# One attention in another order of its heads, and the last stage of the last sequence in two halves

## The reference

```python
# layer 0: causal attention (16 heads of 16), feed-forward with exact gelu, gate
x1 = x + attn(layernorm(x)) @ Wo + bo
x  = x + g * (x1 + gelu(ln(x1) @ W1 + b1) @ W2 + b2 - x)
# layer 1: adapter with an expert chosen per sequence;  layer 2: feed-forward with an expert chosen per sequence
# layer 3: attention with a bias and a mask for every head, then a feed-forward
x = ln(x) * (1 + scale) + shift                  # scale, shift from the timestep
scores = q @ k.T / 4 + attention_bias            # bias: [4, 16, 512, 512] fp32
probs  = softmax(where(src_mask, -inf, scores))
x = x + (probs @ v) @ Wo + bo
h = ln(x) * g2 + beta2
x = x + gelu2(h @ W1 + b1) @ W2 + b2             # W1: 256 x 1024, W2: 1024 x 256; gelu2(z) = z * sigmoid(1.702 z)
```

## Time and profile before

| | |
|---|---|
| three timed runs | 1167.12, 1172.2 and 1169.03 us, median 1169.03 us |
| the profiled execution | 1163.56 us, its span 1161.5 us |
| busy in the span | PE 997.7 us (86%), DVE 730.8 us (63%), ACT 694.2 us (60%), POOL 454.1 us (39%) |
| chain that ended last | PE 51%, DVE 18%, ACT 15%, issue 9%, DMA 4%, POOL 4% |
| HBM | 132 GB/s over the span |
| granted TensorE clock | mean 0.959 of full speed |

### The profile page before, as it was taken

How to read it: one execution, slowest core, us unless ns; L and a number is a source line. 1 busy time by engine, 2 the same in 40 slices (tenths; PEclk the granted TensorE clock), 3 DMA queues, 4 the chain that set the end, 5 groups by cost and what they waited for, 6 DMA issues and landing times.

```text
span 1161.5 us, 22288 instructions
## 1 busy us (share of the span) xinstructions
PE 997.7 (86%) x7668; PEld 658.7 (57%) x7668; DVE 730.8 (63%) x1964; ACT 694.2 (60%) x1608; POOL 454.1 (39%) x694
## 2 busy tenths in 40 slices
PE   4878889897889898798889998897996899799768
PEld 3435557465556575466546565575573557557545
DVE  5677773737755738846773668638649864764750
ACT  3566564664675755676565755656754775675731
POOL 8300020000530374561072006847737564894920
PEclk8899999998999998899999999899897899999989
DMA  6868425133261634854626128575393387944600
GB/s 175 224 157 187 74 73 113 34 84 62 63 140 46 146 122 127 198 177 149 130 75 148 37 90 209 183 166 194 104 226 104 121 225 224 219 141 150 214 1 19
DMA packets 118354, 154.79 MB, mean 133 GB/s; under 512 B 12956, under 2 KB 80924, under 8 KB 118244
## 3 DMA queue, kind: packets, MB, share of 16 engines
q1 hardware_dynamic: 113636, 147.04, 47.3%
q0 software_dynamic: 1936, 3.97, 1.4%
q10 hardware_dynamic: 2672, 2.36, 0.6%
HBM read 134.47 MB, written 18.88 MB: 132 GB/s over the span
## 4 chain that ended last, share of the span: by engine, by line
PE 51%; DVE 18%; ACT 15%; issue 9%; DMA 4%; POOL 4%; DVEq 0%; ACTq 0%; POOLq 0%
PE bank L1307 14%; PE bank L1296 9%; PE bank L1399 7%; PE bank L1258 5%; PE bank L1413 5%; PE bank L1381 4%; POOL bias L798 4%; DMA bias<-in_fside_Bx16xSxS 3%; DVE mrow L1142 3%; ACT gT L874 3%; DVE bias L1148 3%; ACT bias L827 2%; ACT prob L824 2%; ACT L874 2%; ACT L827 2%
## 5 line engine op out<-in xcount | busy, mean ns | idle before, releaser
L798 POOL TENSOR_TENSOR bias<-bias,negmask 128x256 f32<-128x256 f32 x512 | 335.9, 687 | 259.2 <-DMA bias<-in_fside_Bx16xSxS 252.6
L827 ACT ACTIVATE bias<-bias,mrow 128x512 f32<-128x512 f32 x256 | 184.1, 719 | 209.3 <-DVE mrow L1148 207.8
L1148 DVE CUSTOM_DVE_ANT_0 bias<-bank,bias 128x512 f32<-128x512 f32 x256 | 175.4, 687 | 186.5 <-PE bank L1381 175.3
L824 ACT ACTIVATE prob<-bank,mrow 128x128 f32<-128x128 f32 (+3 forms) x256 | 134.7, 527 | 193.1 <-DVE mrow L1142 191.6
L1142 DVE TENSOR_REDUCE mrow<-bank 128x1 f32<-128x128 f32 (+3 forms) x256 | 124.5, 488 | 164.5 <-PE bank L1384 163.1
L1381 PE MATMUL bank<-ks,qs 128*128 128x512 bf16 (+3 forms) x512 | 180.3, 352 | 49.2 <-ACT prob L824 34.5
L1399 PE MATMUL bank<-ident,bias 128*128 128x128 f32 x1024 | 164.7, 286 | 54.0 <-ACT pT L835 43.8
L1399 PEld LDWEIGHTS bank<-ident,bias 128*128 128x128 f32 x1024 | 125.2, 146 | 123.9 <-ACT bias L827 71.3
L1296 PE MATMUL bank<-hT,w 128*128 128x512 f32 x384 | 182.6, 606 | 2.0 <-ACT hT L851 0.9
L1307 PE MATMUL bank<-w,gT 128*128 128x256 f32 x768 | 174.3, 381 | 0.0
L1307 PEld LDWEIGHTS bank<-w,gT 128*128 128x128 f32 x768 | 142.5, 190 | 20.2 <-issue 2.7
(11 more groups left out here) (155 smaller groups left out, 1140.6 us busy)
## 6 DMA issues: line engine op xcount, KB each, us to landing
bias<-in_fside_Bx16xSxS SPq DMA_DIRECT2D x128, 512.0 KB, 4.6
w<-in_L_cond_W SPq DMA_DIRECT2D x16, 1024.0 KB, 5.6
qs<-q_parts SPq DMA_DIRECT2D x30, 384.0 KB, 10.3
ks<-k_parts SPq DMA_DIRECT2D x30, 384.0 KB, 11.7
q_parts<-parts SPq DMA_DIRECT2D x80, 128.0 KB
k_parts<-parts SPq DMA_DIRECT2D x48, 128.0 KB
w<-in_L_cond_Wi SPq DMA_DIRECT2D x4, 1024.0 KB, 5.0
w<-in_L_cond_Wo SPq DMA_DIRECT2D x4, 1024.0 KB, 5.6
```

The lines of the kernel that those rows point to most:

```text
L798: pool.tensor_tensor(b_n, b_n, negmask[:, t, keys], ALU.add).then_inc(masked, 1)
L824: act.activation(prob_of(U), score_bank[U % 2][:, 0:n], ACT.Exp, bias=mrow[:, U % ROW_RING:U % ROW_RING + 1], accum_out=rsum[:, U % ROW_RI ...
L827: act.activation(prob_of(U), prob_of(U), ACT.Exp, scale=-1.0, bias=mrow[:, U % ROW_RING:U % ROW_RING + 1], accum_out=rsum[:, U % ROW_RING: ...
L1148: v.tensor_tensor_reduce(out=prob_of(U), in0=score_bank[U % 2][:], in1=prob_of(U), scale=-1.0, scalar=3e38, op0=ALU.add, op1=ALU.min, accu ...
```

## The change

The last attention goes through its batches as (c 0, tiles 0-1), (c 1, tiles 0-1), (c 1, tiles 2-3), (c 0, tiles 2-3). So `ctxn` of tiles 0 and 1, all heads, is complete 39 ticks after its start. A new plan, `plan_half`, does projection, norm, turn and `hidden` with gelu for tokens 0 to 255 from tick 488 on (448 + 40), beside the rest of the attention, and the same for tokens 256 to 511 from tick 520 on (448 + 72). The products with W2 of the first half come at ticks 521 and 522, behind the second projection. They go to three PSUM banks that the attention used. Stores are three, on SP's queue: tiles 0-1, tile 2, tile 3. SP issues the second `stack` of attention 7 at tick 449. The mask tiles 2 and 3 are turned when batch 2 comes to them.

```diff
+LAST_ATT = len(ATTENTIONS) - 1
+LAST_ORDER = [(0, 0), (1, 0), (1, 2), (0, 2)]
+HALF_AT = [40, 72]
+def plan_half(t, s, i):
+    at(t, "pe", "project", s, 1, i)
+    at(t + 1, "v", "residual", s, 1, i)
+    at(t + 2, "v", "stats", s, 6, i)
+    for r in range(RSQRT_STEPS):
+        at(t + 3 + r // SLOTS, f"v{r % SLOTS}", "rsqrt", s, 6, r, i)
+    at(t + 6, "v", "apply", s, 6, i)
+    at(t + 7, "p", "res_l3_half", s, i)
+    at(t + 7, "pe", "turn_half", s, i)
+    at(t + 8, "v", "feature_cols", s, i)
+    at(t + 8, "a", "feature_cols", s, i)
+    t += 10
+    ahead = (0, 0, 1, 3, 4, 5, 7, 8) if i else range(NF)
+    behind = (1, 1, 1, 5, 5, 5, 8, 8) if i else range(1, NF + 1)
+    for j, (dt, da) in enumerate(zip(ahead, behind)):
+        at(t + dt, "pe", "hidden_cols", s, i, j)
+        at(t + da, "a", "gelu_cols", s, i, j)
+    if i == 0:
+        t = UNITS * LAST_ATT + HALF_AT[1]
+        for x in range(2):
+            at(t + 1 + x, "pe", "ff_out", s, 2, x)
+        at(t + 9, "v", "ff_add", s, 2, 0)
+        at(t + 10, "sp", "store_part", s, 0)
+    else:
+        for x in range(2):
+            at(t + 9 + x, "pe", "ff_out", s, 2, 2 + x)
+            at(t + 10 + x, "v", "ff_add", s, 2, 1 + x)
+            at(t + 11 + x, "sp", "store_part", s, 1 + x)
-STACKS_AT = [(-2, 11)] + [(-28, 4)] * 2 + [(-20, 4)] + [(-28, 4)] * 3 + [(-20, 4)]
+STACKS_AT = [(-2, 11)] + [(-28, 4)] * 2 + [(-20, 4)] + [(-28, 4)] * 3 + [(-20, 1)]
-    [(9, norm(6), 3), (15, block3, 3)],
+for _i, _t in enumerate(HALF_AT):
+    plan_half(UNITS * LAST_ATT + _t, LAST_SEQ, _i)
-A_LOAD = {"feature_half": 7, "hi": 7, "mid": 7, "gelu": 10, "down": 20, "expert": 6}
+A_LOAD = {"feature_half": 7, "feature_cols": 4, "hi": 7, "mid": 7, "gelu": 10, "gelu_cols": 8, "down": 20, "expert": 6}
...
             c, t, e, j = u // (2 * NT * GH), u // (2 * GH) % NT, u // GH % 2, u % GH
+            if a == LAST_ATT:
+                c, t = LAST_ORDER[u // BATCH][0], LAST_ORDER[u // BATCH][1] + u // (2 * GH) % 2
...
+            def store_part(s, i):
+                sp.wait_ge(ff_done, 2 * FFN[s, 2] + i + 1)
+                tt = LAST_TILES[i]
+                sp.dma_start(out[s].rearrange("(t p) d -> p t d", p=P)[:, tt, :], xy[s][:, tt, :]).then_inc(stored, 16)
...
+            def res_l3_half(s, i):
+                pool.wait_ge(tok[5], NT * NTH[s, 5] + 2 * (i + 1))
+                for t in (2 * i, 2 * i + 1):
+                    res(pool.tensor_tensor(xy[s][:, t, :], xy[s][:, t, :], b2[1][:], ALU.add))
+                res_landed()
...
-                    if c == 0 and e == 0 and j == 0:
+                    if e == 0 and j == 0 and (c, t) in ([(0, 0), (0, 1), (1, 2), (1, 3)] if a == LAST_ATT else [(0, x) for x in range(NT)]):
...
+            def gelu_cols(s, i, j):
+                n, cols = FFN[s, 2], slice(HALF * i, HALF * (i + 1))
+                act.wait_ge(f1_psum, NF * (n + i) + j + 1)
+                act.activation(gT[:, j, cols], dense_bank[FF_BANK[j]][:, cols], ACT.Gelu_apprx_sigmoid,
+                               bias=b1[2][:, j:j + 1]).then_inc(g_done, 1)
...
             def ff_add(s, f, i):
+                if (s, f) == (LAST_SEQ, 2):
+                    tt = LAST_TILES[i]
+                    psum = pairs(last_bank[i])[:, 0:tt.stop - tt.start, :]
+                    v.wait_ge(res_pool, res_count(s, 3, min(i, 1)))
...
+            def turn_half(s, i):
+                dense_banks_free(issued)
+                pe.wait_ge(wo_done, 2 * LAST_ATT + i + 1)
+                for t in (2 * i, 2 * i + 1):
+                    pe.wait_ge(tok[5], NT * NTH[s, 5] + t + 1)
+                    for c in range(ND):
+                        mm = pe.transpose(dense_bank[c][:, t * P:(t + 1) * P], h[:, t, c * P:(c + 1) * P], ident[:])
+                mm.then_inc(t_psum, 1)
+            def hidden_cols(s, i, j):
+                n, cols = FFN[s, 2], slice(HALF * i, HALF * (i + 1))
...
+                if j >= 3:
+                    pe.wait_ge(g_done, NF * (n + i) + j - 2)
+                for c in range(ND):
+                    mm = pe.matmul(dense_bank[FF_BANK[j]][:, cols], w1[:, c, j * P:(j + 1) * P], hT[:, c, cols],
+                                   start=c == 0, stop=c == ND - 1)
+                mm.then_inc(f1_psum, 1)
+            def last_out(s, t):
...
+                    pe.wait_ge(max_done, ALL_UNITS)
+                    copied(ALL_UNITS)
+                for j in range(NF):
+                    if t % 2 == 0:
+                        pe.wait_ge(g_done, NF * (n + t // 2) + j + 1)
+                    mm = pe.matmul(last_bank[i][:, (t == 1) * D:((t == 1) + 1) * D],
+                                   gT[:, j, t * P:(t + 1) * P], w2[:, j, :], start=j == 0, stop=j == NF - 1)
...
             def project(s, l, i):
-                if i == 0:
+                if ATT[s, l] == LAST_ATT:
+                    dense_banks_free(issued)
+                    if i:
+                        pe.wait_ge(g_done, NF * (FFN[s, 2] + 1))
+                    pe.wait_ge(ctx_norm, BATCHES * LAST_ATT + 2 * (i + 1))
...
-                if U == 2 * HH or U % (UNITS // 2) == 0 and U:
+                if U == 2 * HH or U % UNITS in ((0, BATCH) if a == LAST_ATT else (0, UNITS // 2)) and U:
                     pe.wait_ge(stack_in[hd // HH], 96 * (a + 1))
```

More of the change, by code:

```diff
@@ L246, in plan_loads @@
 def plan_loads():
-    ffns = sorted((first_tick("pe", "hidden", s, f), s, f) for s in range(B) for f in range(3))
+    ffns = sorted((first_tick("pe", "hidden_cols" if (s, f) == (LAST_SEQ, 2) else "hidden", *((s,) if (s, f) == (LAST_SEQ, 2) else (s, f))), s, f)
+                  for s in range(B) for f in range(3))
     for n, (_, s, f) in enumerate(ffns):
@@ L289 @@
 TURN = order("pe", "turn_tokens", lambda a: a)
+TURN[LAST_SEQ, 5] = len(TURN)
 NTH = {(s, k): sum(1 for x in TURN if x[1] == k and TURN[x] < n) for (s, k), n in TURN.items()}
+NTH[LAST_SEQ, 5] = sum(1 for x in TURN if x[1] == 5) - 1
 FFN = order("pe", "hidden", lambda a: a[:2])
+FFN[LAST_SEQ, 2] = len(FFN)
 QKV = order("pe", "qk", lambda a: a[:2])
@@ L522, in res_count @@
                                            if e == "p" and st.startswith("res")):
-                total += NT * (2 if step == "res_l0" else 1)
+                total += {"res_l0": 2 * NT, "res_l3_half": NT // 2}.get(step, NT)
                 if step == name and args[0] == s:
+                    return total
+                if step == "res_l3_half" and (s, layer) == (LAST_SEQ, 3) and args[1] == half:
                     return total
@@ L852, in feature_half, with feature_cols @@
                                    bias=norm_w[w][:, 2:3]).then_inc(hT_a, 1)
+            def feature_cols(s, i):
+                cols = slice(HALF * i, HALF * (i + 1))
+                act.wait_ge(t_psum, TURN[s, 5] + 1 + i)
+                act.activation(hT[:, 0, cols], dense_bank[0][:, cols], ACT.Identity, scale=norm_w[2][:, 0:1],
+                               bias=norm_w[2][:, 2:3]).then_inc(hT_a, 1)
             def hi(s, l, i):
@@ L1000, in _, with rsqrt @@
             chain = [0]
-            def rsqrt(s, k, i):
+            def rsqrt(s, k, i, half=None):
                 var, bits, guess, sq = nwt[:, 0, :], nwt[:, 1, :], rstd, nwt[:, 2, :]
@@ L1007, in rsqrt @@
                 if i == 0:
-                    for t in range(NT):
+                    tiles = range(NT) if half is None else range(2 * half, 2 * half + 2)
+                    for t in tiles:
                         count[0] += 1
                         ins = v.bn_aggr(mv[:, t, :], stats[:, t, :])
-                        if t < NT - 1:
+                        if t < tiles[-1]:
                             ins.then_inc(vec, 1)
@@ L1170, in normalize @@
                 a, b = divmod(p, BATCHES)
-                c, t = b // 2, b % 2 * 2
+                c, t = LAST_ORDER[b] if a == LAST_ATT else (b // 2, b % 2 * 2)
                 if b == 0 and a:
@@ L1284, in project @@
                 mm.then_inc(wo_psum, 1)
-                if i == 1:
+                if i == 1 and ATT[s, l] != LAST_ATT:
                     issued["out"] += 1
@@ L1427, in _ @@
             steps = dense_steps("pe")
-            do = {"turn_tokens": turn_tokens, "qk": qk, "v": v_rows, "project": project, "hidden": hidden,
+            do = {"turn_tokens": turn_tokens, "turn_half": turn_half, "hidden_cols": hidden_cols, "qk": qk, "v": v_rows, "project": project, "hidden": hidden,
                   "ff_out": ff_out, "turn_expert": turn_expert, "down": down, "expert": expert, "up": up, "setup": setup, "restack": restack}
```

45 lines of the change are left out of this document (34 added, 11 removed).

## The result

The changed kernel took 1185.3 us (median of four runs, 1176.27 to 1190.37) beside 1168.07 us for the kernel before on the same chip: ratio 1.0135, 95% interval 1.0077 to 1.0193. Six more runs in the first experiment gave 1181.95 us, ratio 1.0114 (1.0090 to 1.0139). Forecast were 1172.5 us and a range of 1164 to 1180, so the loss, 13.5 to 17 us, is four to five times the forecast 3.6. The profiled execution took 1176.27 us with a span of 1174.5, 13.0 us more than before.

The account below looks back on a forecast made before the run. It took POOL's mask additions to bound the last attention, with nothing overlapping in the 46.5 us behind it. Terms 1.5 + 22.2 - 0.5 - 19.6 + 0 = +3.6 us; on the median 1172.5 us, range 1164 to 1180.

Parts of the forecast that it names:

- The table loads of the middle: Ticks 499 to 506: one gelu a tick beside an exponential, eight Gelu and eight Exp loads; added 22.2 us, bounds 21.3 and 23.8.
- rival 4: Each of the 16 table loads holds ACT once more for its own length, 1.28: +20.5 us, 1193; chance 0.03.
- rival 3: Tables don't switch tick by tick; gelus grouped as in sequence 2, three load pairs for eight: -12.8 us, 1160; chance 0.05.
- The tail: From the last ctxn to the end of the span: 19.6 us saved, some 2.9 of it from the clock.
- The order and the mask tiles: Last attention: the two mask tiles move to ticks where POOL waits for bias anyway; cost 0.
- Ticks 488 to 498: First half's projection, norm, transposes and hT beside the last attention: cost 1.5 us, POOL's two additions; bounds 0 and 5.
- DVE gets about 5 us: DVE's added work in ticks 488 to 498, against slack of 3.3 and copies worth 2.3 going to ACT: it fits.
- PE gets about 1.8 + 1.0, within its slack over 11 units: PE's added projection and transposes in ticks 488 to 498 fit its slack of some 0.3 us a unit.
- Ahead of it: Second stack of attention 7 issued at tick 449, not 452, some 4 us sooner: cost 0, bounds -4.3 and +2.
- Rival 2: Earlier stack removes POOL's 4.29 us bias wait, so sequence 2's stage begins sooner: -2.2 us in all, 1166.8; chance 0.16.
- rival 1: Low clock: half-idle PE in the eight slow ticks leaves the last units and tail's start at 1.2 GHz: 1177.5; chance 0.28.
- The base: Sum 1167.2 us against the profiled execution, plus 5.5 by which the median of timed runs exceeded it: 1172.6.

Follow-up runs that it names:

- the first experiment: The changed kernel timed again with nothing altered, to see how far its runs lie apart: 1181.95 us, ratio 1.0114 to the kernel before.

## Why the prediction was wrong

*The table loads of the middle*: right. The step had 22.2 us, the trace has 21.5; with three pairs in place of eight 14.8 us went (13.2 of them in units 499 to 507). A load has no drain behind it (1110.62 to 1111.91, 1.29 us), so rival 4 falls, and rival 3 as well.

*The tail*: right, 19.6 us in both, clock included. *The order and the mask tiles*: right, nothing.

*Ticks 488 to 498*: wrong, 1.5 against 7.8 us (5.7 to 7.8 in nine profiles), and the upper bound of 5 too low. Three steps failed:

- "DVE gets about 5 us", and with it "So DVE's sum fits". I took DVE's durations from the earlier trace rows, the norm behind the attention, where POOL stands still, and put them beside a POOL that is busy 27.2 of 28 us. With POOL kept quiet DVE's busy time in this stretch grew by 2.4 us (11.97 to 14.35), which is the 5 less the 2.3 of the copies; with POOL at work it grew by 5.4 (to 17.41). That put 3.0 us on the path. I looked at each engine's slack alone, not at two engines that slow each other.
- "PE gets about 1.8 + 1.0, within its slack over 11 units". The projection is one lump at one tick, and 1.8 us of it stood on the path in every kernel that has it there. The prediction itself had said that a lump on one engine doesn't fit.
- The clock in these ticks was not in the sum at all. Behind the norm it was low in the first profile and cost some 2.1 us.

*Ahead of it*: wrong, 0 with bounds -4.3 and +2 against +3.5 in the profile, and +4.1 between the means of seven and six profiles. The failing step is "I take 0, since the bytes stay the same", with the +2 that bounds "pairs held up ahead of it can lengthen another". The stack went 5.9 us sooner (992.32 for 998.20), where I had some 4. The bytes did stay the same and the pair behind the stack came as late as before after its issue, but it was now the pair of unit 458, for which DVE stood waiting: 1.9 us in this profile, up to 4.9 in others; what makes it vary so is not shown. The wait of 4.29 us that "An earlier start can shorten" had cost little where it was, since DVE did most of the norm of sequence 2 under it, at 0.16 us a step. Rival 2, the earlier stack frees the stage ahead, had the sign reversed: unit 458 comes 2.1 us later after unit 448, not sooner.

*The clock*: rival 1 had the place wrong. Low clock came in the slow ticks, as it said, with PE busy 17.9 of 30 us, and cost nothing there. It went with lost time behind the norm of the first half, from 1095 to 1102. It was low from 1013 to 1027 too, but there the wait for the bias pair came first.

*The base*: the forecast put its sum on one profiled execution and one median. The changed kernel's two medians are 9.0 and 5.7 us above its first profiled execution, where the kernel before had 5.5. For the six later runs a profile shows where the time went: 6.2 us ahead of unit 448. For the other three of the first four runs (1183.87 to 1190.37, mean clock 0.947 to 0.951) there is no profile; where they lost their time stays open.

These steps are the miss: +7.8 and +3.5 where I had 1.5 and 0. Together with the terms that were right they give the 13.0 us of the profile, near the 13.5 of the six later runs.

## What to carry to other kernels

Price DVE's small SBUF operations beside a busy POOL by rows in which POOL is busy: here half of them took 0.59 and not 0.16 us, whatever DVE's own slack. A wait for a DMA costs what its readers have to do meanwhile: before you move a large transfer ahead, find the transfer that will now stand behind it, and ask what the engine that waits for it does in that time. Don't spread a lump of one engine over the slack of many ticks. Work that needs another ACT table belongs in few groups, best behind the last use of the first table; parking its inputs in free PSUM halves made that possible here, and together with the stack back at 452 turned a loss of 1.1% into a gain of 1.0%. Take more than one profile of a kernel before you read a difference of 2 us in one stretch.

## What the hardware showed

- A DVE instruction of 128x4 fp32 or int32 from SBUF took 0.15 to 0.18 us with POOL quiet, and for the most part 0.52 to 0.69 us under a continuous row of POOL tensor_tensor of 128x256, with shorter ones in between; the fused sum and extreme of 128x512 with scores in PSUM took 0.67 to 0.69 us in both.
- ACT_TABLE_LOAD took 1.283 us in each of the changed kernel's 37 loads for gelu_cols and the layer 3 exponential, with 0.01 us to the next ACTIVATE.
- A gelu of 128x256 took 0.47 us alone and some 0.38 in a row of six.
- At the low clock the same row of 32 products with the values took 1.94 us, and 1.08 at the full one; four transposes of 128x128 took 1.06 us, and 0.60 in the tail.
- A bias pair of 512 KB issued right behind the six stack DMAs landed 14.5 to 14.8 us after its issue; the median of all bias pairs was 4.6.
